# A decoder of ten sections on one core: the weight loads of later sections move from SP's queue to ACT's, one step later

## The reference

```python
x = _layernorm(x + _L0_attn_ref(x, ...))      # causal attention, 16 heads of 16, one key head
x = _layernorm(x + _L0_xattn_ref(x, ctx, ctx))# attention over channels
x = _layernorm(x + _L0_ffn_ref(x, ...))       # integer weights, dequantised, 704 hidden
x = _layernorm(x + _L1_attn_ref(x, ...))      # 16 query heads that share one key head
x = _layernorm(x + _L1_xattn_ref(x, ctx, ctx, gamma))  # attention over positions
x = _layernorm(x + _L1_ffn_ref(x, ...))       # ternary weights, quantised input
x = _layernorm(x + _L2_attn_ref(x, ...))      # cumulative attention and SwiGLU
x = _layernorm(x + _L2_xattn_ref(..., x, ctx))# decayed running sum over the sequence
x = _layernorm(x + _L2_ffn_ref(x, ...))       # fp8 linear layer
x = _layernorm(x + _L3_attn_ref(x, ...))      # ALiBi attention, 16 heads of 128
x = _layernorm(x + _L3_xattn_ref(x, ctx, mask, ...))   # 16 query, 4 key heads of 128
x = _layernorm(x + _L3_ffn_ref(x, ...))       # ternary weights, GELU, 1024 hidden
return x
```

## Time and profile before

| | |
|---|---|
| median of 3 runs | 4915.02 us |
| the profiled execution | 4917.29 us |
| its span in the profile | 4915.3 us |
| PE busy | 4447.4 us (90%) |
| DVE busy | 3261.4 us (66%) |
| ACT busy | 2048.8 us (42%) |
| POOL busy | 1522.7 us (31%) |
| mean granted TensorE clock | 0.975 |
| DMA, mean over the span | 23 GB/s, 8.3% of 16 engines |

### The profile page before, as it was taken

The page is one execution under the profiler, slowest core; times in us unless marked ns, Lnnn a source line. Parts: engine busy times, 40 slices in busy tenths (PEclk is TensorE's granted clock), DMA queues, the critical chain, the costliest instruction groups (busy, mean ns, idle before and its releaser), DMA issues.

```text
span 4915.3 us, 87683 instructions
## 1 busy us (share of the span) xinstructions
PE 4447.4 (90%) x32598; PEld 3090.8 (63%) x32645; DVE 3261.4 (66%) x6084; ACT 2048.8 (42%) x4390; POOL 1522.7 (31%) x3050
## 2 busy tenths in 40 slices
PE   8998998799989898887799999999978999999788
PEld 6776887455546676776466666666655666666555
DVE  5667227788877678877555555555546666666798
ACT  4554113355544333333355555555533434343222
POOL 1111004433312233433344444444422222222122
PEclk9999998899999999999899999999999999999899
DMA  1003001344410100000000000000010000000000
GB/s 44 2 25 91 1 1 24 95 88 88 88 43 25 73 7 7 7 9 6 31 1 1 1 1 1 1 1 1 1 42 18 9 7 9 7 9 4 6 14 17
DMA packets 117700, 111.69 MB, mean 23 GB/s; under 512 B 22368, under 2 KB 110112, under 8 KB 112800
## 3 DMA queue, kind: packets, MB, share of 16 engines
q1 hardware_dynamic: 117280, 106.09, 8.3%
HBM read 88.48 MB, written 16.78 MB: 21 GB/s over the span
## 4 chain that ended last, share of the span: by engine, by line
PE 58%; issue 15%; DVE 15%; POOL 7%; ACT 4%; DMA 1%; SPq 1%; POOLq 0%; DVEq 0%; ACTq 0%
PE banks L2421 14%; PE banks L1279 5%; PE banks L2671 4%; PE banks L769 4%; POOL factors L2883 3%; PE banks L1910 3%; PE banks L1262 3%; PE banks L1155 2%; PE banks L2487 2%; PE banks L798 2%; PE banks L2587 1%; PE banks L1816 1%; PE banks L523 1%; PE banks L2515 1%; POOL mean_squares L2879 1%
## 5 line engine op out<-in xcount | busy, mean ns | idle before, releaser
L282 POOL TENSOR_TENSOR var_eps<-mean_var,ln_eps 128x1 f32<-128x1 f32 x384 | 83.3, 217 | 1309.2 <-DVE mean_var L278 959.3
L1319 ACT ACTIVATE exps<-banks 128x512 f32<-128x512 f32 x512 | 284.9, 595 | 259.1 <-PE banks L1262 258.9
L1167 DVE TENSOR_REDUCE neg_max<-banks 128x4 f32<-128x1024 f32 x256 | 311.2, 1217 | 98.4 <-PE banks L1155 98.1
L2442 ACT ACTIVATE squares<-banks 128x512 f32<-128x512 f32 x256 | 152.8, 597 | 441.4 <-PE banks L2421 441.4
L2475 DVE TENSOR_TENSOR q_normed<-banks,factors 128x512 f32<-128x512 f32 x256 | 176.3, 689 | 229.6 <-POOL factors L2465 229.3
L2859 ACT ACTIVATE squares<-q_normed 128x512 f32<-128x512 f32 x160 | 100.8, 630 | 396.6 <-DVE q_normed L2849 396.6
L2465 POOL TENSOR_TENSOR factors<-mean_squares,minus_half 128x4 f32<-128x4 f32 x256 | 258.5, 1010 | 21.5 <-POOL mean_squares L2461 0.3
L1910 PEld LDWEIGHTS banks<-yT,w_swiglu 128*128 128x128 f32 x2048 | 238.0, 193 | 30.0 <-issue 29.8
L1910 PE MATMUL banks<-yT,w_swiglu 128*128 128x128 f32 x2048 | 247.2, 277 | 8.4 <-DVE hidden L1934 8.4
L2421 PE MATMUL banks<-wq,x_turned 128*128 128x512 f32 x512 | 249.0, 609 | 3.0 <-ACT x_turned L2401 1.9
L284 POOL TENSOR_TENSOR rstd<-var_eps,minus_half 128x1 f32<-128x1 f32 x384 | 242.0, 630 | 30.1
(11 more groups left out here) (381 smaller groups left out, 11050.2 us busy)
## 6 DMA issues: line engine op xcount, KB each, us to landing
contextT<-in_ctxT SPq DMA_DIRECT2D x96, 128.0 KB, 2.5
parts_context<-parts SPq DMA_DIRECT2D x96, 64.0 KB, 2.2
parts_x<-parts SPq DMA_DIRECT2D x96, 64.0 KB, 2.0
stack<-parts_context SPq DMA_DIRECT2D x32, 192.0 KB
stack<-parts_x SPq DMA_DIRECT2D x32, 192.0 KB
x_all<-in_x SPq DMA_DIRECT2D x1, 4096.0 KB, 14.2
context<-in_ctx SPq DMA_DIRECT2D x64, 64.0 KB, 2.2
context<-in_ctx SPq DMA_DIRECT2D x32, 128.0 KB, 2.3
```

The costliest lines, as they stand in the source:

```text
L1167: v.tensor_reduce(self.mx[s][:, :, 2 * i:2 * i + 2].rearrange("p h g -> p g h"), self.bM[i % 2].rearrange("p g (h c) -> p g h c", h=DH), A ...
L1319: self.nc.scalar.activation(self.e[n % 8][:], self.bE[self.slot(t, n) % 2].rearrange("p (l c) -> p l c", l=DH), ACT.Exp, scale=self.TOK ** ...
```

## The change

ACT issues the loads in place of SP: `walk` has the wait and the loads in ACT's program, after step `done_at[k]`, and `done_at` grows by one step, or by one tile's worth of ticks where a section counts in ticks (8 in section 6, 12 in section 7, 8 in section 8). Which tensors are loaded, where they go and who waits for them stays, as do the loads of sections 0 and 1, which SP issues at the start.

```diff
                     step(eng, name, k, n)
-                    if name == "sp" and n == done_at[k]:
+                    if name == "act" and n == done_at[k]:
                         finished(eng, k - 1)
                         if k + 1 < len(SECTIONS):
                             load(eng, k + 1)
 
-        def load(sp, k):
+        def load(eng, k):
             for stage in sections[k]:
-                stage.issue_loads(sp)
-
-
-        done_at = [None] + [len(section[4] or ()) for section in SECTIONS[1:]]
+                stage.issue_loads(eng)
+
+
+        done_at = [None] + [len(section[4] or ()) + max(1, stages[0].TICKS) for section, stages in zip(SECTIONS[1:], sections[1:])]
```

## The result

The changed kernel took 4939.23 us, the median of 5 runs (4934.63 to 4942.47), against 4914.54 of the kernel before in the same measurement: +24.7 us, a ratio of 1.0049 (95% interval 1.0036 to 1.0063). It is slower by more than the 0.2% of the prediction. 4933.5 was forecast, +18.5, in a range from 4901 to 4944, and from 4926 to 4944 for the likeliest case alone.

The account below looks back on a forecast made before the run. PE carried 58% of the chain of waits, but a few stalls around the load points were to decide. The terms summed to +18.5 us: 4917.3 profiled became 4935.8, and 4933.5 as median, range 4901 to 4944.

Parts of the forecast that it names:

- Section 1: Tile 11's scores no longer wait for context behind seven loads, -8.7 us; ACT's time issuing them, +0.8.
- Section 5: ACT's six issues take 7.0 us, and nearly all of it shows in a loop without deep buffer: +6.5 us.
- Section 6: ACT held by nine issues, 15.23 us in `q_weight` alone; PE stops, then runs at half clock: +21.8 us.
- Section 8: 2 MB of loads from ACT run beside `wo` and the first context, which lands later: +5.3 us.
- Section 4: Tile 1's score no longer waits for moves behind three loads, -8.7 us; ACT's issues and slowed tile 2 moves, +1.0.
- Rival C: Slower than forecast: stalls of sections 1 and 4 go only by half, up to 4942 us; chance 0.10.
- Section 2: ACT's issues take 6.55 us, but the gates between are PE's input later: 0, bounds 0 and +1 us.
- section 7: Three issues on ACT, 1.5 us, in a section of many short waits: +0.3 us, bounds 0 and 1.5.
- Rival A: Faster: ACT's compute isn't held by its DMA issues, decided in section 6; 4902.9 us, chance 0.18.
- Rival B: About no change: the seventh load in section 6 doesn't block at ACT, issues take about 0.45 us; 4911 us, chance 0.12.

Follow-up runs that it names:

- the repeat: The changed kernel measured and profiled once more with no edit: 4942.36 us, ratio 1.0051 to the kernel before (4915.35 us).

## Why the prediction was right

It forecast slower, by 18.5 us; +24.7 and +27.0 were measured, inside the range, and the repeat's 4942.36 close to its end. Part of the nearness is luck: the first profile comes to +17.6 only because -4.4 us at the start, ahead of any moved load, and -2.4 in section 3, 0.0 in the second profile of the same kernel, stand against the term that was too small. One sum of the forecast is off as well: with sections 5 and 8 at 0 the low end is 4933.5 - 6.5 - 5.3 = 4921.7, and not 4926.

**Sections 1, 5, 6 and 8** went by their steps. Section 1: -8.7 + 0.8 forecast, -7.6 in both traces; 3.2 of it come with the later step alone, the rest by leaving SP's queue. Section 5: +6.5 against +6.2 and +6.6. Section 6: +21.8 against +21.6 and +21.8; it rested on the reading that SP's 15.23 us would be ACT's too, and the issue took 15.81. The cost is right, the reason given for it isn't: the prediction read the hold as a queue that is full until the 8 MB ahead have gone, and with the same 8 MB in another order no issue took over 0.57 us. Section 8: +5.3 against +4.6 and +4.4, sections 8 and 9 together (with this section alone +5.7 by the medians and +3.7 in the trace). That these are causes, and not only stages in which time went, is shown by the runs with one part each: section 6 back at SP, -18 to -21; 5 and 6 alone, +25.9; 8 alone, +5.7; 1 and 4 alone, -10.5. No run has section 1 alone.

**Section 4 is the step that failed.** Its cost was put at +1.0, with +3.4 as the bound, since "3 MB now run beside tile 2's moves of 8 KB"; +6.2 and +8.4 were measured. I had taken over half of the wait of tile 1 as the most that could return. Tile 2 waited 4.41 and 5.31 us, and what they cost beyond the waits (1.8 and 3.1) goes with PE's slower clock behind them (granted 0.57 from 926 to 930 us in the first profile; 0.50 and then 0.66 from 935 to 943 in the second), as 2.6 of the 8.7 did in the gain; the bound counted the wait alone. This term, 5.2 and 7.4 too small, is most of the difference between +18.5 and the measured +24.7 to +27.0. Nor did the -8.7 come by leaving SP's queue: the run with only the step moved has the same gain and the same stall at tile 2. Gain and cost are one stall that moved on by a tile. Rival C was true, then, in section 4, and false in section 1.

**The other small terms.** Section 2 showed +1.0 and +0.6 and section 7 +1.6, where 0 and 0.3 were forecast. The +1.0 and +0.6 come at 461 us, ahead of section 2's loads, and +1.0 and -0.2 stand there in the two kernels whose loads in section 2 are SP's and in section 1 ACT's; with both at SP it is 0.1 to 0.2. So section 2's loads cost 0, as forecast, and what makes the +1 stays open. Of section 7's 1.6 us, 1.1 come in its last 12 us (3655 to 3668), where the two kernels with the same loads at ACT (section 6 back to SP, small tensors first) show -1.7. So these aren't the loads' either.

**Rival A** (ACT's compute goes on through its issues) is refuted: the tanh of tick 18, due at once, started 19.45 us after the work before it, 0.10 us after the last issue ended, and with shorter issues that idle shrank to 3.98 us (4.44 us of issues). Work placed ahead of the loads does run on: in section 1 three exponentials start at 369.08 to 369.98, after the first load went out at 368.65. The sentence of the Trainium skill on instructions that are read and queued while the sequencer executes ("Advanced Engine Details and Errata", "Sequencer and Instruction Queues") isn't borne out by the trace for compute placed behind a held DMA issue: that isn't started. **Rival B** (no held issue at ACT) fell by the 15.81 us, but is nearly what sections 5 and 6 do with the small tensors first (2.2 and 6.3 us against its 2.7 and 3.8).

## What to carry to other kernels

In these runs a DMA issue costs the engine that issues it the time for which the queue holds it, and that isn't always the 0.4 us of a free one: look in the old queue for the longest issue (15 us here) before moving it to an engine that computes. Here the issues behind one tensor of many short rows were held, and putting that tensor last, with nothing more to issue from that engine, took the hold away; the order of loads is worth a trial before their engine is changed. And where large loads delay small urgent transfers, try the loads one per step, right behind the urgent ones, from the queue that they are in: this won 14 us where the move to ACT lost 25 to 27.

## What was unexpected of the hardware

Executions of the changed kernel lie between 4933.35 and 4946.17 us, and part of such a spread is how long PE stays at half clock after a short wait. Around 325 us PE waits for the same contextT in the kernel before and in the changed one, 4.55 and 4.58 us. Windows of both, 324 to 328 and 328 to 332 us, first the kernel before, then the changed one:

```profile
324.00:328.00 4.00, 4.00 (x18) 2.82 (x20) 0.00 (x0) 0.00 (x0) 0.00 (x0) 0.50 0.51 144
328.00:332.00 4.00, 4.00 (x60) 3.81 (x59) 0.00 (x0) 0.00 (x0) 0.00 (x0) 0.50 0.38 103
```

```profile
324.00:328.00 4.00, 4.00 (x69) 3.31 (x69) 0.00 (x0) 0.00 (x0) 0.00 (x0) 0.78 0.51 149
328.00:332.00 4.00, 3.48 (x29) 2.79 (x28) 2.50 (x6) 1.98 (x4) 1.34 (x3) 1.00 0.19 56
```

After the same wait the granted clock was back at 1.00 (2.4 GHz) from 328 us on in the changed kernel and stayed at 0.50 (1.2 GHz) up to 332 us in the kernel before, where the next 64 matmuls (L523) took 3.61 us in place of 2.05. This made 3.4 of the 4.4 us in the first row of the table, and it is part of why the first profile stood 7 us nearer to that of before (17.3) than the medians do (24.7). In the repeat's profile PE did as in the kernel before (3.61 us for the same 64 matmuls).
